# Joining the last stage to the scan's program in a vision tower with a two-way selective scan

## The reference, cut to what matters

```python
h = h + attn(layernorm(h))     # a selective scan (Mamba) forwards and one backwards over the 5 tokens
h = h + ffn(layernorm(h))      # one of 8 experts per token

# attn: for each direction
h_s = da * h_s + dbu           # state, 16 per channel, 512 channels, 5 steps
y   = einsum('bdn,bn->bd', h_s, c) + xc * D_skip
out = (y * silu(z)) @ out_w.T  # the two directions are averaged

# ffn
scores = x @ gate_w.T;  chosen = argmax(scores)
out = x + expert_w[chosen] @ x
```

## Time and profile before

| | us |
|---|---|
| median of 3 runs | 537.95 (536.87 to 539.11) |
| the profiled execution, its own time | 537.0 |
| its span, first to last instruction | 535.2 |
| TensorE busy | 484.4 (91%) |
| VectorE busy | 380.0 (71%) |
| ScalarE busy | 237.7 (44%) |
| GpSimd busy | 171.3 (32%) |

### The profile page before, as it was taken

One profiled execution on the slowest core, in us unless ns is written; L12 is line 12 of the kernel. 1 busy time (PEld: TensorE's weight loads), 2 busy tenths in 40 slices (PEclk: granted clock), 3 DMA queues, 4 the chain that ended last, 5 costly groups with the idle time before them and its releaser, 6 DMA issues. The chain is left out here.

```text
span 535.2 us, 6853 instructions
## 1 busy us (share of the span) xinstructions
PE 484.4 (91%) x1812; PEld 237.1 (44%) x1812; DVE 380.0 (71%) x718; ACT 237.7 (44%) x416; POOL 171.3 (32%) x163
## 2 busy tenths in 40 slices
PE   6989999999999998996879568989999998989997
PEld 3545555555555465543546312222222222376653
DVE  0066576575566677653999759999999999287655
ACT  1112213212222311659969537788878888121100
POOL 6000100100100112222250016888888888242000
PEclk9999999999999999999588959999999999999999
DMA  9981009300000000500334765665557565400000
GB/s 267 308 263 41 1 5 318 97 1 1 1 1 0 0 1 1 149 0 0 104 103 131 213 185 146 163 193 149 165 148 202 144 169 158 118 4 12 10 11 20
DMA packets 36426, 53.55 MB, mean 100 GB/s; under 512 B 5652, under 2 KB 27184, under 8 KB 36402
## 3 DMA queue, kind: packets, MB, share of 16 engines
q1 hardware_dynamic: 35746, 52.52, 34.3%
q10 hardware_dynamic: 656, 0.73, 0.4%
HBM read 35.83 MB, written 17.27 MB: 99 GB/s over the span
## 5 line engine op out<-in xcount | busy, mean ns | idle before, releaser
L1686 POOL TENSOR_TENSOR gb<-da,hb 128x512 f32<-128x512 f32 x94 | 117.1, 1281 | 65.8 <-ACT da L1622 65.8
L1716 DVE TENSOR_TENSOR da<-ps,expA 128x512 f32<-128x512 f32 x128 | 84.9, 683 | 10.1 <-PE ps L1520 8.9
L304 PE MATMUL ps<-xbuf,convw 128*128 128x384 f32 (+1 forms) x240 | 82.9, 499 | 4.8 <-DMA convw<-in_conv_wT 4.8
L1622 ACT ACTIVATE da<-da 128x512 f32<-128x512 f32 x128 | 78.0, 626 | 17.0 <-DVE da L1716 14.7
L358 PE MATMUL ps<-wall,peT 128*128 128x512 f32 x144 | 67.8, 593 | 0.0
L1520 PE MATMUL ps<-drows,selb 96*128 96x512 bf16 x128 | 50.5, 400 | 16.3 <-DMA drows<-dparts 10.5
L304 PEld LDWEIGHTS ps<-xbuf,convw 128*128 128x128 f32 (+1 forms) x240 | 46.0, 194 | 36.7 <-ACTq L501 4.0
L1532 PE MATMUL ps<-urows,brows 96*128 96x512 bf16 x128 | 48.8, 399 | 1.4 <-DVE gb L1723 0.8
L528 ACT ACTIVATE kvs<-ps 128x512 f32<-128x512 f32 x36 | 21.5, 597 | 57.4 <-PE ps L358 57.4
L520 ACT ACTIVATE peT<-ps 128x384 f32<-128x384 f32 x24 | 11.8, 491 | 75.4 <-PE ps L304 75.4
L1734 DVE TENSOR_TENSOR hb<-gb,ps 128x512 f32<-128x512 f32 x64 | 42.0, 676 | 0.0
(11 more groups left out here) (218 smaller groups left out, 746.4 us busy)
## 6 DMA issues: line engine op xcount, KB each, us to landing
xbuf<-in_xT SPq DMA_DIRECT2D x11, 768.0 KB
yscr<-yst SPq DMA_DIRECT2D x30, 208.0 KB
brows<-bparts SPq DMA_DIRECT2D x16, 240.0 KB, 3.3
uparts<-pt SPq DMA_DIRECT2D x24, 128.0 KB, 2.4
dparts<-pt SPq DMA_DIRECT2D x24, 128.0 KB, 2.4
drows<-dparts SPq DMA_DIRECT2D x15, 192.0 KB, 2.7
urows<-uparts SPq DMA_DIRECT2D x15, 192.0 KB, 3.2
inw<-in_in_wT SPq DMA_DIRECT2D x2, 1024.0 KB
```

What stands on the lines that cost most here:

```text
L304: mm = pe.matmul(bank(T_EMB + j % 2, 0, EN), convw[0:n, k, h * P:(h + 1) * P], xbuf[0:n, q, k, c * EN:(c + 1) * EN], start=(k == 0), stop= ...
L1622: act.activation(da_at(q, j), da_at(q, j), ACT.Exp, scale=-1.0).then_inc(da_ready, 1)
L1686: pool.tensor_tensor(gb_at(q, j), da_at(q, j), hb[:, s_ - 2, d, :], ALU.mult).then_inc({2: m2_done, 3: m3_done, 4: m4_done}[s_], 1)
L1716: dve.tensor_tensor(da_at(q, j), bank(j % 2), expA[:, j % 2, :], ALU.mult).then_inc(e_free, 1)
```

## The change

1. The last stage's engine programs become functions (`finish_tensor`, `finish_scalar` and so on) that are called behind `scan_...` in the same `nc.Block`. TensorE gets waits for the PSUM banks that it takes over (`e_free`, `bu_used`, `y_copied`, `m4_done`). The first token's sums count on a semaphore of their own, `first_summed`.
2. `keep_clock` is gone.
3. Groups 14 and 15 both go within SBUF (`send_y`, four DMAs of 16 KB), and `gather_y` brings only groups 0 to 13 and waits only for the store of group 13. k = 0 is sent by SyncE, k = 1 by ScalarE's queue. Group 15 gets a buffer of its own, `ylast`, so that its copies wait for no store.
4. In group 15 the step "3" is VectorE's (`last_decayed`), not GpSimd's.

```diff
+        Y_ORDER = [(2, 3, 0, 1), (3, 2, 1, 0)]
+        def send_y(eng, src, g, k):
+            eng.wait_ge(y_copied[k], g + 1)
+            for j in Y_ORDER[k]:
+                d, s_ = j % 2, 2 * k + 1 + j // 2
+                t = token(s_, d)
+                eng.dma_start(ytok[g * GB:(g + 1) * GB, d, t, :], src[32 * j:32 * j + GB, k, :]).then_inc(y_landed[t], 16)
...
             def gather_y(k):
-                sp.wait_ge(y_stored[k], 16 * (NG - 1))
-                for j in range(4):
+                sp.wait_ge(y_stored[k], 16 * (NG - 2))
+                for j in Y_ORDER[k]:
...
-                    if last and q == 1:
-                        last_y(0)
+                    if last and q == 0:
+                        send_y(sp, yst, g, 0)
+                    elif last:
+                        send_y(sp, ylast, g, 0)
                     else:
                         store_y(g, 0)
                     if last and q == 0:
+                        store_y(g - 1, 1)
                         gather_y(0)
-                    if not (first and q == 0):
+                    elif last:
+                        gather_y(1)
+                    elif not (first and q == 0):
                         store_y(g - 1, 1)
-                    if last and q == 1:
-                        gather_y(1)
             pairs(sp, body)
-            last_y(1)
...
             def add_decayed(g, q, d):
-                pe.wait_ge(m3_done, 2 * g + d + 1)
+                if isinstance(g, int) and g == NG - 1:
+                    pe.wait_ge(last_decayed, d + 1)
+                else:
+                    pe.wait_ge(m3_done, 2 * g + d + 1)
...
             pairs(pe, body)
             add_decayed(NG - 1, 1, 1)
-            pe.wait_ge(w_landed, W_ALL)
-            pe.wait_ge(e_free, 2 + 8 * NG)
-            keep_clock(6)
             outputs(NG - 1, 1, 1)
-            keep_clock(3)
...   (ScalarE, scan)
             def copy_y(g, k):
                 act.wait_ge(y_done[k], g + 1)
+                if isinstance(g, int) and g == NG - 1:
+                    act.activation(ylast[0:NY, k, :], bank(6 + k, p=NY), ACT.Copy).then_inc(y_copied[k], 1)
+                    return
                 act.wait_ge(y_stored[k], 16 * g)
...
                     if not (first and q == 0):
                         copy_y(g - 1, 1)
+                    if last and q == 1:
+                        send_y(act, yst, g - 1, 1)
...
             copy_y(NG - 1, 1)
+            send_y(act, ylast, NG - 1, 1)
...   (GpSimd, scan)
-                    for d in range(2):
-                        decayed(g, q, 3, d)
+                    if not (last and q == 1):
+                        for d in range(2):
+                            decayed(g, q, 3, d)
...   (VectorE, behind the scan's loop)
+            for d in range(2):
+                dve.wait_ge(bu_used, 2 + 6 * (NG - 1) + 4 + d + 1)
+                dve.wait_ge(da_ready, 8 * (NG - 1) + 4 + d + 1)
+                dve.wait_ge(y_done[1], NG - 2)
+                dve.tensor_tensor(gb_at(1, 4 + d), da_at(1, 4 + d), hb[:, 1, d, :], ALU.mult).then_inc(last_decayed, 1)
...
+        def finish_tensor(pe):
...
+            pe.wait_ge(e_free, 2 + 8 * NG)
+            turned(0)
+            pe.wait_ge(w_landed, W_ALL)
+            pe.wait_ge(bu_used, 2 + 6 * NG)
+            projected(0)
+            turned(1)
+            projected(1)
+            turned(2)
+            pe.wait_ge(y_copied[1], NG)
+            x_turned(0)
+            projected(2)
+            pe.wait_ge(m4_done, 2 * NG)
+            pe.wait_ge(y_copied[0], NG)
+            for n in range(L):
...
         with nc.Block() as block:
             @block.tensor
             def _(pe):
                 prepare_tensor(pe)
                 scan_tensor(pe)
+                finish_tensor(pe)
```

More of the change, by code:

```diff
@@ L1351, in tower, with y_sum @@
         NIL = ((0, 0), (L - 1, 1))
-        def y_sum(eng, d, t):
+        def y_sum(eng, d, t, done):
             if (t, d) not in NIL:
-                eng.wait_ge(y_landed[t], 32 if t in (0, L - 1) else 64)
-                eng.tensor_tensor(skip[:, d, t, :], skip[:, d, t, :], ytok[:, d, t, :], ALU.add).then_inc(sum_done, 1)
+                eng.wait_ge(y_landed[t], 48 if t in (0, L - 1) else 96)
+                eng.tensor_tensor(skip[:, d, t, :], skip[:, d, t, :], ytok[:, d, t, :], ALU.add).then_inc(done, 1)
         d_landed = [sem(f"d_landed{q}") for q in range(2)]
@@ L1464, in gather_y @@
             def gather_y(k):
-                sp.wait_ge(y_stored[k], 16 * (NG - 1))
-                for j in range(4):
+                sp.wait_ge(y_stored[k], 16 * (NG - 2))
+                for j in Y_ORDER[k]:
                     d, s_ = j % 2, 2 * k + 1 + j // 2
                     t = token(s_, d)
[L1469 to L1478, removed]
+                    sp.dma_start(ytok[0:(NG - 2) * GB, d, t, :],
+                                 yscr[0:NG - 2, k, 32 * j:32 * j + GB, :]).then_inc(y_landed[t], 16)
             def load_outw(k):
@@ L1825, in tower, with finish_sync, finish_gpsimd, root @@
                                                             sem("o_stored"), sem("f_chain"))
-        with nc.Block() as block:
+        def finish_sync(sp):
+            for t in range(L):
+                sp.wait_ge(mo_ready, t + 1)
+                sp.dma_start(out[:, ORDER[t], :], mo[:, t, :]).then_inc(o_stored, 16)
+            sp.wait_ge(o_stored, 16 * L)
+        def finish_gpsimd(pool):
+            def root(n):
+                pool.wait_ge(fve_ready, n + 1)
+                pool.tensor_tensor(frs[:, n:n + 1], fve[:, n:n + 1], mhalf[:, 0:1], ALU.pow).then_inc(frs_ready, 1)
+            for n in range(1, L):
+                for d in range(2):
+                    y_sum(pool, d, ORDER[n], sum_done)
+                if n == 2:
+                    root(0)
+                if n == 3:
+                    root(1)
+            for n in range(2, L):
+                root(n)
@@ new lines, in finish_scalar, with copy_y, copy_x @@
+        def finish_scalar(act):
+            def copy_y(n):
+                for d in range(2):
+                    act.wait_ge(ygt_ready, 2 * n + d + 1)
+                    if n >= 2:
+                        act.wait_ge(o_ready, n - 1)
+                    act.activation(ygT[:, n % 2, d, :, :], bank(d), ACT.Copy).then_inc(ygt_copied, 1)
+            def copy_x(n):
+                act.wait_ge(xt5_ready, n + 1)
+                if n >= 2:
+                    act.wait_ge(ex5_ready, 4 * (n - 1))
+                act.activation(xfT[:, n % 2, :, :], bank(7, 0, C), ACT.Copy).then_inc(xt5_copied, 1)
+            for n in range(3):
+                copy_y(n)
+            copy_x(0)
+            for n in range(1, L):
+                copy_x(n)
+                if n + 2 < L:
+                    copy_y(n + 2)
@@ new lines, in tower, with _ @@
+        with nc.Block() as block:
+            @block.tensor
+            def _(pe):
+                prepare_tensor(pe)
+                scan_tensor(pe)
+                finish_tensor(pe)
+            @block.scalar
+            def _(act):
+                prepare_scalar(act)
+                scan_scalar(act)
+                finish_scalar(act)
+            @block.gpsimd
+            def _(pool):
+                prepare_gpsimd(pool)
+                scan_gpsimd(pool)
+                finish_gpsimd(pool)
+            @block.vector
+            def _(dve):
+                prepare_vector(dve)
+                scan_vector(dve)
+                finish_vector(dve)
@@ L1827, in _ @@
             @block.sync
             def _(sp):
[L1829 to L1902, removed]
-                    if n >= 1:
-                        x_turned(n)
-                    if n >= 1 and n + 2 < L:
-                        turned(n + 2)
-                    experts(n)
-                    if n >= 1 and n + 2 < L:
-                        projected(n + 2)
```

216 lines of the change are left out of this document (111 added, 105 removed).

## The result

Over 15 runs each, taken side by side, the kernel before has a median of 538.85 us (535.53 to 543.7) and the changed one 534.38 us (530.82 to 539.5). The ratio is 0.9925, 95% interval 0.9896 to 0.9954: 4.0 us faster, 2.5 to 5.6. The prediction was 534.0 us, within 531.0 to 536.5.

What follows compares the result with a forecast made beforehand. TensorE was taken to bound the kernel from the last stage on, its start held by the seam. From 537.0, 4.65 and 1.6 us saved and 2.3 lost to the clock give 533.05; median 0.95 higher, 534.0 us, range 531.0 to 536.5.

Steps and rivals of the forecast that it cites:

- TensorE bounds the last stage, so the seam counts one for one: Last stage: TensorE is the bound from 469.56, so starting that stage sooner moves the end by as much.
- Part 1: End of scan: without filling products and with step 3 on VectorE, the last outputs start 4.65 us earlier.
- Part 2: Last sends and program end: from ScalarE's copy to the first projection 3.4 us instead of 5.0, 1.6 us earlier.
- Part 3: Seam without fillers: TensorE's clock falls for 3.3 to 5.9 us and 2.3 us are lost.
- The sum: Whole kernel: 537.0 - 6.25 + 2.3 = 533.05, with the median 0.95 higher, so 534.0 us.
- Part 4: Last stage: token 0, wanted at 468.3, has landed by 465 and is gated by 468.05, so it just fits.
- The clock holds: Rival at the seam: no fall of the clock, 531.7 us; chance 0.17.
- a clock of 1.00 throughout: Sign at the seam that the prediction is wrong: the granted clock never reads 0.5.
- Clock low through the projections: Rival in the last stage: clock rises only at the experts, 15 us lost, 546.7 us; chance 0.08.
- Token 0 late: Rival at projection 1: token 0's data lands late, projection 1 starts 2 us late, 536.0 us; chance 0.08.

Runs made afterwards that it cites:

- the fillers in the idle time: The changed kernel with unread 512-column products, one behind the last outputs and two behind the first transposes; ratio 0.9907 to the kernel before.
- the split sends: The changed kernel with only token 0's k=1 send of group 15 on ScalarE, the other three on SyncE; ratio 0.9910 to the kernel before.
- the last two kernels of the table: Changed kernel, three of group 15's k=1 sends on SyncE, one unread product, gathers of tokens 0 and 4 early; second also token 0's sum on VectorE: 0.9872, 0.9858.
- the split kernels: Two kernels: changed kernel with three of group 15's four k=1 sends on SyncE, without and with one unread product; ratios 0.9910 and 0.9904 to before.

## Why the prediction was right, point by point

**TensorE bounds the last stage, so the seam counts one for one: right.** From projection 1 to the end of the span there are 59.5 us before (535.2 - 475.72) and 60.3 after, the 0.8 us being the last store's; to VectorE's end it is 57.3 in both. It isn't so in every variant: where the gating of tokens 0 and 4 ended after projection 1 had started and the clock stayed up, the first experts took 0.3 to 0.8 us longer, in three of four by a wait for VectorE (the fillers in the idle time, the split sends, and the last two kernels of the table).

**Part 1, outputs 4.65 us sooner: right in place and size** (4.75, 8.58 to 3.83). VectorE's step took 1.98 us for two beside GpSimd, hidden as worked out. But the part was credited to the fillers, and that fails as a statement about them: taken out alone they brought 1.0 us at the transposes, and the clock took it back. What I had not seen in the earlier trace rows is that SyncE's chain of store, landing, gather and sends would have ended at the same time. In the sum it didn't matter, because the change removes both.

**Part 2, 1.6 us: right in place, 0.2 to 0.5 us too large where the clock fell.** ScalarE's four issues took 2.62, 2.86 and 3.08 us in the three profiles, so SyncE's price of 2.73 for the same transfer was the right row. Copy end to projection was 3.4 us (463.36 to 466.80), as said, in the first, 3.7 and 3.9 us in the others, against 5.0 before. Group 14's sends ended 0.2 us before the last outputs did in the first profile and 0.4 us in the others, not 0.5.

**Part 3, the clock, 2.3 us: right in kind, too large.** It fell in two of three profiles of the changed kernel, and cost 1.69 us each. The low stretch was 3.4 us, at the short end of what I allowed (3.3 to 5.9): I took a middle between stretches whose work was transposes and 33-row products, while here dense products follow. How often it falls can't be said closely; the mean clocks fit most executions. The seam gained 6.37 us to projection 1 where the clock held, 4.2 to 4.4 where it fell. With the 0.3 to 0.8 us that the end behind VectorE's last instruction took longer in these profiles that is 5.6 and 3.7 to 3.9 us. The timed 4.0 (2.5 to 5.6) agrees with the latter; the former is at its edge.

**The sum: right, with some luck.** Where the clock fell, 4.75 from part 1, 1.1 to 1.4 from part 2 and 1.69 lost to the clock give the 4.2 to 4.4 at projection 1. The forecast of 3.95 met the timed 4.0 so closely because its 0.6 us too much for the clock stood in for the issues, taken 0.2 to 0.5 us too cheap, and for the end, which is 0.3 to 0.8 us longer and wasn't in the sum. Why the end behind VectorE's last instruction takes 2.2 us in some profiles and up to 3.0 in others stays open.

**Part 4, token 0 just fits: right in the outcome, its landing too short.** The prediction allowed 3.1 us from issue to landing and called the limit 3.3. The sum began 3.6, 4.9 and 4.2 us after the issue in the three profiles of the changed kernel, and yet its transposes followed projection 0 without a gap, twice with the slow projection 0 giving it time. The reading behind the 3.1 us was weak: the traffic at 468 to 469 can be that of the four last sends, which were issued until 468.61, and need not be the gather's. In the split kernels token 0 became the bound, with 4.7 and 5.0 us.

**Rivals.** The clock holds: true in one profile of three, which shows one of the prediction's own signs of being wrong, a clock of 1.00 throughout. Clock low through the projections: refuted by each fall: even after 7.6 us of idle (the kernel before without fillers) the clock was back at 1.00 within projection 0, with 128x256 products only. Token 0 late: latent, shown in the split kernels.

## What to carry to other kernels

Before an edit is priced by the wait it removes, follow the second chain into the same point: here two of nearly equal length met at the end of a program. Removing one paid nothing, removing both paid 2.0 us (0.7 to 3.3), and with the meeting point gone as well it was 4 us. A DMA issued from a compute engine's queue costs that engine its issue time each (0.63 to 0.77 us here), so put there only the one whose data is wanted first. After taking away products that kept TensorE busy, look for the next short idle stretch; where it was filled with work that fits into it, the clock held in the one profile taken, and projection 0 came no later for it.

## What the runs showed of the hardware that I had not expected

An idle stretch of little over 2 us between small products can be followed by a halved clock: 2.28, 2.50, 2.17 and 2.12 us were, 2.04 in the first profile of the changed kernel and 2.35 in the split one weren't. Its length alone doesn't decide: at the same place between token 0's transposes 2.12 us was followed by a fall and 2.35 us, in a kernel with one unread product less ahead, was not. In the five profiles with idle stretches of 2.1 to 3.1 us the fall came 0.4 to 1.4 us after the dense products had begun. The Trainium skill, TensorE: Matmul & The Clock Gate, section "HAM oscillation — how this bites in real kernels", warns only of longer idle than any of these; the measurements decide. Each of these five falls was over after 3.4 us and cost 1.6 to 1.7 us of a projection. Where the clock fell during longer idle, 4.72 and 7.60 us, it was low for 6.8 and 10.2 us, and the transposes ahead of the projection were slow too: 2.6 and 2.2 us in all (1.94 and 5.43 or 5.06 us against 1.06 and 3.69 or 3.72).

A 16 KB transfer within SBUF took 2.1 us from issue to the sum that waited for it when the last gather had been issued 3.1 us before, 3.2 to 3.4 us when two gathers of 224 KB ran near it, and 3.6 to 5.1 us with four of them issued just ahead. The Trainium skill, DMA: Bandwidth & Descriptors, section "Issuing engines are not separate DMA queues", says just that of the shared engines; but the issue times it calls usually small were 0.63 to 0.77 us each on ScalarE's queue here (2.62 to 3.08 for four), and bounded the seam.
